# Fourteen turns per step of a gated-delta-rule kernel: from TensorE and ScalarE to DMA from buffer to buffer

## What is computed

```python
x = layernorm(x + attention(x))          # 16 key heads, 32 value heads, head size 128
x = layernorm(x + ffn(x))                # 12 experts of 256 x 640 x 256, all computed, weighed per token
# attention, per head pair: projection, causal convolution of 4 taps, silu, rms norm of q and k, then
def step(S, (q, k, v, g, beta)):         # over 512 tokens
    S = S * exp(g);  delta = (v - k @ S) * beta
    S = S + outer(k, delta);  return S, q @ S
# rms norm of the outputs, gate silu(z), projection W_out
```

## Time and profile before

| | us |
|---|---|
| median of 3 runs | 1567.07 (1566.12 to 1569.17) |
| the profiled execution's own time | 1565.32 |
| its span | 1563.5 |
| TensorE busy in the span | 1456.9 |
| VectorE busy | 1132.9 |
| ScalarE busy | 1064.0 |
| GpSimd busy | 701.1 |
| a walk of ORDER in the middle of the run | 67.6 |
| VectorE's copy of su 0 to St (line 895), first and last of 16 | 135.9 and 1135.8 |

### The profile page before, as it was taken

One profiled execution on the slowest core, in us unless ns is written; L12 is line 12 of the kernel. 1 busy time (PEld: TensorE's weight loads), 2 busy tenths in 40 slices (PEclk: granted clock), 3 DMA queues, 4 the chain that ended last, 5 costly groups with the idle time before them and its releaser, 6 DMA issues. The chain is left out here.

```text
span 1563.5 us, 38623 instructions
## 1 busy us (share of the span) xinstructions
PE 1456.9 (93%) x14982; PEld 1174.2 (75%) x14982; DVE 1132.9 (72%) x1970; ACT 1064.0 (68%) x2130; POOL 701.1 (45%) x613
## 2 busy tenths in 40 slices
PE   3589999999999999999999999999977899999994
PEld 2368898888988889888888989888864556656574
DVE  2588999999999999989999998999745332313214
ACT  2467878778787878778778887877635455464640
POOL 1243555454455544545454545545324344353530
PEclk9799999999999999999999999999998899999997
DMA  3000102021110202111020110202213111111100
GB/s 110 1 1 22 35 22 56 2 56 22 35 36 23 55 9 49 30 29 38 20 56 16 43 35 22 56 2 42 35 21 98 51 35 67 34 34 67 34 0 27
DMA packets 100713, 55.70 MB, mean 36 GB/s; under 512 B 74556, under 2 KB 93000, under 8 KB 100552
## 3 DMA queue, kind: packets, MB, share of 16 engines
q1 hardware_dynamic: 100552, 53.47, 13.9%
HBM read 35.62 MB, written 1.05 MB: 23 GB/s over the span
## 5 line engine op out<-in xcount | busy, mean ns | idle before, releaser
L819 DVE SCALAR_TENSOR_TENSOR con<-bank,taps,con 128x1022 f32<-128x1022 f32 (+2 forms) x192 | 245.2, 1277 | 24.0 <-ACT con L612 19.4
L1459 POOL TENSOR_TENSOR h<-h 128x512 f16<-128x512 f32 x120 | 146.2, 1226 | 177.8 <-ACT h L1278 171.5
L968 POOL TENSOR_TENSOR gl<-const_sb,gc 128x512 f16<-128x512 f32 x128 | 129.8, 1041 | 184.5 <-DVE gc L826 98.7
L1400 DVE SCALAR_TENSOR_TENSOR facc<-bank,gcol,facc 128x256 f32<-128x256 f32 x96 | 42.0, 479 | 224.4 <-PE bank L1193 224.4
L351 PE MATMUL bank<-x,qkv 128*128 128x512 f16 x768 | 184.6, 392 | 17.5 <-DVE con L819 13.6
L1179 PE MATMUL bank<-y,w 128*128 128x512 f16 x720 | 168.2, 384 | 6.4 <-ACT h L1278 3.3
L1277 ACT ACTIVATE h<-bank,b 128x512 f32<-128x512 f32 x120 | 82.5, 688 | 127.1 <-PE bank L1179 124.3
L1193 PE MATMUL bank<-w,h 128*128 128x256 f16 x1440 | 161.8, 275 | 2.4 <-DVE w L1323 2.4
L1193 PEld LDWEIGHTS bank<-w,h 128*128 128x128 f16 x1440 | 142.0, 99 | 23.1 <-DVE w L1323 2.6
L874 DVE TENSOR_TENSOR X<-X,bank 128x512 f16<-128x512 f16 x192 | 130.0, 683 | 32.4 <-PE bank L441 30.9
L351 PEld LDWEIGHTS bank<-x,qkv 128*128 128x128 f16 x768 | 75.0, 102 | 101.2 <-DVE con L819 14.9
(11 more groups left out here) (209 smaller groups left out, 3889.6 us busy)
## 6 DMA issues: line engine op xcount, KB each, us to landing
w<-in_w SPq DMA_DIRECT2D x24, 640.0 KB, 4.5
w_qkv<-in_W_qkvz SPq DMA_DIRECT2D x16, 512.0 KB, 3.9
w_z<-in_W_qkvz SPq DMA_DIRECT2D x16, 256.0 KB, 2.8
w_out<-in_W_out SPq DMA_DIRECT2D x16, 256.0 KB, 3.0
Z<-in_xT SPq DMA_DIRECT2D x1, 1024.0 KB, 5.3
y<-in_x SPq DMA_DIRECT2D x1, 1024.0 KB, 10.0
sqo<-oo SPq DMA_TRANSPOSE x64, 3.1
out_dram<-y SPq DMA_DIRECT2D x8, 128.0 KB, 1.8
```

The lines of the kernel that those rows point to most:

```text
L819: stt(out=out, in0=bank[:, 0:B, 0:S - k], scalar=taps[:, par, t, TAPS - 1 - k:TAPS - k], in1=out, op0=ALU.mult, op1=ALU.add).then_inc(tap_ ...
L968: last = tt(gl[:, g % 2, k].rearrange("p (m r) d -> p m r d", m=2), upper.unsqueeze(1).unsqueeze(1).broadcast_to([P, 2, R, P]), gc[:, par, ...
L1459: tt(h16[:, par, 1, t, at], h32[:, k % H32], h16[:, par, 0, t, at], ALU.subtract)\
```

## The change

1. Each x0 and turn becomes one DMA on SP's queue, from X0 to Z0 for eight matrices, with a semaphore `turned[h]` for each half. TensorE's transposes and ScalarE's copies of them go, and the PSUM banks that they took. All of Z0 is now written at each level. `p_level` and `apply_once` on TensorE wait for `turned`, and `start` on VectorE waits for it before X0 is written again.
2. The masks of levels 4 and 5 ("y") go from VectorE to ScalarE: with b = 32 the mask is constant along each run of 32 columns, with b = 64 along all 64, so a Copy with a scale from one mask column does it: two instructions of 8 x 32 columns at level 4 and one of 8 x 64 at level 5, for each half.
3. The copy of su's bank to St for chunk 0 goes from VectorE to ScalarE.
4. ORDER and BANK are new. Among other things "kk" 0 and 1, "aT" 0 and 1 and "decay" 1 end the walk (a = 2) where they were at its beginning or end with other a, "turn" (5, 1), "once" 2 and "split" z begin it, and the weights of head n are loaded up to three walks ahead (DEEP is 3, it was 2).

```diff
+TURNS = 16 * (LEVELS + 1)
+        turned = [sem(f"turned{h}") for h in range(2)]
@@ sync
+                def turn(h):
+                    sp.dma_start_transpose(out=Z0[:, 8 * h:8 * h + 8], in_=X0[:, 8 * h:8 * h + 8].rearrange("p u t -> p (u t)"))\
+                        .then_inc(turned[h], 16)
+
+                def turn_start(n, par, h):
+                    is_free(sp, n, ("st", 2 * h), ("st", 2 * h + 1))
+                    is_full(sp, n, ("Z", 2 * h, 1), ("Z", 2 * h + 1, 1))
+                    turn(h)
+
+                def turn_level(n, par, lh):
+                    l, h = lh
+                    is_free(sp, n, ("p", lh))
+                    turn(h)
+
+                run(sp, {"load": load, "oT": tail, "x0": turn_start, "turn": turn_level})
@@ tensor
-                def turn_start(n, par, h):
...
-                    is_free(pe, n, ("y", lh), ("turn", (l - 1, h)) if l else ("x0", h), taking=("p", lh))
+                    is_free(pe, n, ("y", lh), taking=("p", lh))
+                    pe.wait_ge(turned[h], TURNS * n + 16 * l + 16)
-                def turn_level(n, par, lh):
...
-                    is_free(pe, n, ("turn", (LEVELS - 1, g // 2)), taking=("once", g))
+                    pe.wait_ge(turned[g // 2], TURNS * n + TURNS)
@@ scalar
-                def turn_start(n, par, h):
...
-                def turn_level(n, par, lh):
+                def y_level(n, par, lh):
                     l, h = lh
...
+                    if l < LEVELS - 2:
+                        return
+                    is_full(act, n, ("y", lh), ("p", (l - 1, h)))
+                    pairs_of = 2 ** (LEVELS - 1 - l)
+                    for q in range(pairs_of):
+                        cols = slice(q * P // 2 // pairs_of, (q + 1) * P // 2 // pairs_of)
+                        last = do(Y[:, h, :, cols], at_bank("y", lh).rearrange("p (u k) -> p u k", u=8)[:, :, cols], ACT.Copy,
+                                  scale=ymask[:, l, cols.start:cols.start + 1])
+                    freed(last, "y", lh)
+                def su(n, par, c):
+                    if c == 0:
+                        is_full(act, n, ("su", c), ("ks", CH - 1, 1), ("qs", CH - 1, 1))
+                        freed(do(St[:].rearrange("p b r d -> p (b r d)"), at_bank("su", c), ACT.Copy), "su", c)
@@ vector
-                    is_full(dve, n, ("st", g), ("res", g, 1), ("turn", (LEVELS - 1, g // 2), 1))
+                    is_full(dve, n, ("st", g), ("res", g, 1))
+                    if after(n, 1):
+                        dve.wait_ge(turned[g // 2], TURNS * n)
+                    if l >= LEVELS - 2:
+                        return
-                    if c == 0:
-                        is_full(dve, n, ("su", c), ("ks", CH - 1, 1), ("qs", CH - 1, 1))
-                        freed(nc.vector.tensor_copy(St[:].rearrange("p b r d -> p (b r d)"), at_bank("su", c)), "su", c)
-                    else:
+                    if c:
                         is_full(dve, n, ("su", c), ("qs", c))
+                        if c == 1:
+                            is_free(dve, n, ("su", 0))
```

The new ORDER (BANK, which is new throughout, is left out):

```diff
+    (1, "aH", 0), (0, "turn", (5, 1)), (0, "split", "z"), (0, "once", 2),
+    (2, "split", "qkv"), (0, "res", 3), (0, "Z", 2), (1, "st", 0),
+    (1, "aH", 1), (1, "gl", 2), (1, "unit", 0), (1, "kk", 2),
+    (0, "once", 1), (0, "solve", 0), (1, "decay", 2), (1, "pT", 0),
+    (1, "st", 1), (1, "x0", 0), (1, "aT", 2), (0, "Z", 1),
+    (0, "su", 0), (0, "pdl", 0), (1, "aL", 0), (1, "unit", 1),
+    (1, "y", (0, 0)), (3, "load", "qkv"), (0, "sqo", 0), (1, "gl", 3),
+    (0, "ks", 1), (1, "aH", 2), (0, "kd", 1), (1, "decay", 3),
+    (0, "once", 3), (1, "turn", (0, 0)), (1, "p", (0, 0)), (1, "kk", 3),
+    (0, "solve", 1), (1, "aT", 3), (1, "sq", 0), (1, "st", 2),
+    (1, "pT", 1), (1, "aH", 3), (0, "qs", 1), (0, "sum", 0),
+    (0, "load", "out"), (0, "kd", 2), (0, "su", 1), (0, "Z", 3),
+    (1, "unit", 2), (1, "y", (1, 0)), (1, "st", 3), (0, "ks", 2),
+    (1, "x0", 1), (0, "sqo", 1), (1, "aL", 1), (0, "pdl", 1),
+    (1, "p", (1, 0)), (1, "y", (0, 1)), (0, "solve", 2), (0, "qs", 2),
+    (1, "turn", (1, 0)), (0, "sum", 1), (1, "y", (2, 0)), (1, "p", (0, 1)),
+    (1, "turn", (0, 1)), (0, "pdl", 2), (0, "su", 2), (1, "v", (1, 1)),
+    (0, "sqo", 2), (1, "p", (2, 0)), (1, "turn", (2, 0)), (1, "y", (1, 1)),
+    (0, "split", "out"), (0, "sum", 2), (2, "proj", 1), (1, "p", (1, 1)),
+    (0, "ks", 3), (1, "turn", (1, 1)), (1, "v", (1, 0)), (1, "y", (2, 1)),
+    (2, "tap", 1), (0, "qs", 3), (1, "turn", (2, 1)), (0, "solve", 3),
+    (1, "norm", 0), (2, "silu", 1), (0, "pdl", 3), (1, "p", (2, 1)),
+    (1, "pT", 2), (1, "y", (3, 0)), (0, "sum", 3), (1, "turn", (3, 0)),
+    (0, "sqo", 3), (1, "turn", (4, 0)), (2, "proj", 2), (2, "gc", 0),
+    (1, "y", (3, 1)), (1, "p", (3, 0)), (1, "unit", 3), (2, "tap", 2),
+    (1, "turn", (3, 1)), (0, "weigh", 0), (0, "weigh", 1), (2, "tok", 0),
+    (0, "power", 0), (2, "sq1", 1), (2, "tok", 1), (0, "oT", 0),
+    (0, "z", 0), (0, "z", 1), (1, "y", (4, 0)), (2, "silu", 2),
+    (0, "z", 2), (0, "high", 0), (1, "p", (3, 1)), (1, "p", (4, 0)),
+    (0, "oT", 1), (2, "proj", 3), (1, "turn", (5, 0)), (0, "high", 1),
+    (0, "z", 3), (2, "kT", 1), (1, "y", (5, 0)), (2, "tap", 3),
+    (2, "v", (0, 0)), (1, "y", (4, 1)), (2, "kT", 0), (0, "low", 0),
+    (2, "v", (0, 1)), (0, "weigh", 2), (1, "pT", 3), (2, "silu", 3),
+    (0, "low", 1), (1, "p", (5, 0)), (0, "weigh", 3), (2, "proj", 0),
+    (1, "kd", 0), (1, "p", (4, 1)), (1, "turn", (4, 1)), (2, "tap", 0),
+    (1, "aL", 2), (0, "oT", 2), (2, "gl", 0), (0, "high", 2),
+    (1, "res", 0), (0, "op", 0), (0, "high", 3), (1, "load", "z"),
+    (1, "once", 0), (1, "y", (5, 1)), (1, "res", 1), (0, "op", 1),
+    (2, "gl", 1), (2, "silu", 0), (2, "decay", 0), (1, "p", (5, 1)),
+    (1, "Z", 0), (2, "decay", 1), (2, "kk", 0), (2, "aT", 0),
+    (1, "aL", 3), (0, "low", 2), (0, "oT", 3), (2, "kk", 1),
+    (0, "low", 3), (2, "aT", 1), (1, "res", 2), (0, "op", 2),
     (0, "op", 3),
```

More of the change, by code:

```diff
@@ L37 @@
 ORDER = [
[11 rows of a table removed]
-    (1, "aH", 3), (2, "load", "qkv"), (1, "turn", (0, 0)), (1, "unit", 3),
[10 rows of a table removed]
[L60 to L65, removed]
@@ L66 @@
-    (1, "y", (5, 0)), (1, "p", (3, 1)), (2, "tap", 2), (2, "sq1", 1),
-    (0, "weigh", 0), (2, "tok", 0), (2, "tok", 1), (1, "turn", (4, 0)),
[5 rows of a table removed]
[L73 to L77, removed]
@@ L78 @@
-    (1, "res", 2), (1, "Z", 0), (1, "once", 2), (1, "kd", 1),
-    (2, "silu", 0), (1, "aL", 3), (0, "op", 2), (2, "decay", 1),
+    (1, "aH", 0), (0, "turn", (5, 1)), (0, "split", "z"), (0, "once", 2),
[4 more added lines that the diff above has]
+    (0, "su", 0), (0, "pdl", 0), (1, "aL", 0), (1, "unit", 1),
@@ L83 @@
 BANK = {
[11 rows of a table removed]
-    ("solve", 3): 7, ("turn", (3, 0)): 3, ("decay", 0): 4, ("y", (3, 1)): 2, ("pdl", 3): 7,
-    ("p", (4, 0)): 6, ("turn", (2, 1)): 5, ("norm", 0): 3, ("y", (5, 0)): 4, ("p", (3, 1)): 7,
-    ("tok", 0): 6, ("tok", 1): 5, ("turn", (4, 0)): 2, ("z", 0): 3, ("z", 1): 4,
[3 rows of a table removed]
-    ("once", 0): 2, ("p", (5, 1)): 5, ("res", 1): 7, ("op", 1): 6, ("turn", (5, 1)): 5,
-    ("res", 2): 4, ("Z", 0): 3, ("once", 2): 5, ("op", 2): 2, ("decay", 1): 5,
-    ("op", 3): 7,
+    ("once", 2): 7, ("res", 3): 5, ("Z", 2): 3, ("st", 0): 7, ("kk", 2): 2,
+    ("once", 1): 6, ("solve", 0): 4, ("decay", 2): 3, ("st", 1): 6, ("Z", 1): 5,
[15 rows of a table added]
 }
+TURNS = 16 * (LEVELS + 1)
 DEEP = max(a for a, *_ in ORDER)
@@ L311, in tail @@
                                            in_=oo16[:, g].rearrange("p k u d -> p (k u d)")).then_inc(oT_in[g], 16)
-                run(sp, {"load": load, "oT": tail})
+                def turn(h):
[10 more added lines that the diff above has]
+                run(sp, {"load": load, "oT": tail, "x0": turn_start, "turn": turn_level})
             @block.tensor
@@ L442, in p_level @@
                     filled(last, "p", lh)
-                def turn_level(n, par, lh):
-                    l, h = lh
-                    is_free(pe, n, ("p", lh), taking=("turn", lh))
-                    out = half16(take(n, "turn", lh))
-                    for j in range(8):
-                        last = turn(out[:, j], X0[:, 8 * h + j], ident16[:])
-                    filled(last, "turn", lh)
                 def residual(n, par, g):
@@ L556, in _ @@
                 run(pe, {"proj": proj, "norm": norm, "tok": tok, "v": turn_v, "kT": turn_k, "decay": decay_sum,
-                         "kk": products, "st": start, "x0": turn_start, "y": y_level, "p": p_level, "turn": turn_level,
+                         "kk": products, "st": start, "y": y_level, "p": p_level,
                          "res": residual, "once": apply_once, "Z": finish_z, "z": z, "ks": ks, "qs": qs,
@@ L668, in high_part @@
                     do(aH[:, 4 * g:4 * g + 4], aT[:, g % 2], ACT.Copy).then_inc(aH_ready, 1)
-                def turn_start(n, par, h):
```

(16 more changed lines are left out.)

## The result

The changed kernel takes 1598.01 us (1596.52 to 1599.04, 4 runs) against 1568.12 us (1566.12 to 1569.88) before: a ratio of 1.019, interval 1.0174 to 1.0206. It is 30 us slower, where 71 us less were forecast. The profiled execution has a span of 1595.9 us, 32.4 more than before.

A forecast was written before the change was run, and what follows sets the result against it. TensorE was taken as the bound: 61.3 + 1.4 (tap 3) + 0.2 (hops) + 0.1 = 63.0 us a walk, 64 us over 14 walks, plus 4 and 3 at the ends: 71 less, 1496 us. Range 1468 to 1548.

The forecast's parts named there:

- TensorE's list: Walks 0 to 13: TensorE sets the end; without 14 turn blocks its work falls from 67.5 to 61.3 us.
- ScalarE and the masks: Each walk: VectorE falls from 62.45 to 59.4 us; ScalarE gains 3.0, stands at 49 of 61 and hides it.
- Worth by themselves: nothing: Masks and su's copy moved to ScalarE gain no time alone, since TensorE is the bound.
- The order: New ORDER per walk: VectorE is late next, between y (3, 1) and proj 0, 13.6 us against TensorE's 12.2.
- The wait for tap 3: At proj 0, once a walk, TensorE waits 1.4 us for VectorE.
- The hops: From p by VectorE through DMA to the next p: tight ones cost 0.2 us a walk, bounds 0 to 5.4.
- The fit that the prediction quotes: DMA landing: about 2.0 us plus bytes at 436 GB/s, 2.6 us for 256 KB; the trace's 3.1 was used.
- The ends: Outside walks 0 to 13: walk 14 gains 4 us, walk -1 with the first inverse 3, walk 15 nothing.
- The clock, slower: Rival, chance 0.09: waits for landings drop TensorE's mean clock to 0.90, a walk of 69.7 us, time 1596.
- TensorE alone: Rival, chance 0.15: the new order leaves no wait, a walk of 61.4 us, time 1470.
- VectorE bound: Rival, chance 0.18: VectorE's 5.1 us a walk of waits for banks remain, a walk of 64.5, time 1519.
- Late landings: Rival, chance 0.13: landings typically 4.5 us cost about 3 us more, a walk of 66, time 1542.

The follow-up runs named there:

- masks_only: The kernel before with only the masks of levels 4 and 5 and su's first copy moved to ScalarE, old order and TensorE turns: 1567.73 us, 1.0008.
- masks_on_vector: gl_early with the masks of levels 4 and 5 back on VectorE: 1684.33 us, 1.0756 of the kernel before.
- gl_early: The changed kernel with GpSimd's gl 0, gl 1 and VectorE's gc 0 moved forward into GpSimd's idle time: 1553.21 us, 0.9917 of the kernel before.
- no_level_turns: The changed kernel without the twelve level turns, x0's DMAs kept, inverse not the reference's: 1578.87 us, 1.0083 of the kernel before.
- no_turns_gl_early: gl_early with no DMA from X0 to Z0 at all, Z0 filled once with a constant: 1525.35 us, 0.9734 of the kernel before.
- old_order_dma: The changed kernel with ORDER and BANK of before, oT entries moved behind their low: 1752.15 us, 1.119 of the kernel before.

## Why the prediction was wrong

**TensorE's list (change 1).** Right. 67.5 was to fall to 61.3; in the last window above, 63.57 less gaps of 2.5 us, read off block by block from start to start, is 61.1.

**ScalarE and the masks (changes 2 and 3).** The size was right: 49.15 us against 49 (rows below). "Worth by themselves: nothing" is right in the old order (masks_only) and right for the reason given. In the new order ScalarE doesn't hide the masks quite: kT 0 stands 0.47 us a walk for one, 0.6 from start to start, for which the sum had nothing. I did write that they count because VectorE would stand at 62.4; that measured VectorE by its sum. masks_on_vector says that position, not sum, was the point: 6 us a walk of waits, 8 with the clock.

```profile
L677 ACT ACTIVATE Y<-bank,ymask 128x256 f16<-128x256 f32 x64 | 27.1, 487 | 0.0
L677 ACT ACTIVATE Y<-bank,ymask 128x512 f16<-128x512 f32 x32 | 21.9, 685 | 0.0
```

**The order (change 4): the step that failed.** The prediction priced weigh at 1.05 us and VectorE at 59.4 a walk, durations read in the old order, and carried them into a new one without asking what GpSimd does at that moment. I followed TensorE, VectorE, ScalarE and SP through the new ORDER, but not GpSimd, which at 34 of 67 us looked like no bound. It needn't be one to hold up another engine. Weigh 2 and 3 stand on VectorE's path for TensorE: tap 3, weigh 2, the read of p (5, 0), on which res 0 and turn (5, 0) wait, weigh 3, the read of p (4, 1), on which turn (4, 1) waits. Their spans are 3.89 + 2.33 = 6.2 us in place of 2.3. gl_early takes 3.5 of these 4.0 us away, and 3.0 reach the end of the walk: 68.3 to 65.3 (45 us of the time).

The 5.3 us a walk that the forecast was short by are then these 3.0, 1.5 of hops beyond the 0.2 that it took (below), and 0.8 that stay without any turn, ScalarE's mask ahead of kT 0 among them.

The wait for tap 3, forecast at 1.4 us from start to start, was 0.79 idle and 0.95 from start to start in the walk without turns, and 0.15 idle after the change, where TensorE comes late itself.

**The hops.** "I take 0.2 us a walk", with bounds of 0 to 5.4. Measured 1.3 (after against no_level_turns) to 1.7 (gl_early against no_turns_gl_early), within the bounds, but the value taken was too near the lower end. The median landing was 3.1 as taken. (The fit that the prediction quotes beside it from the Trainium skill, "DMA: Bandwidth & Descriptors", Anatomy of one DMA, was measured on GpSimd's DMA queue. These transfers are SP's, none of them landed in under 3.0 us, and the sum rightly went by the trace.) What was missed is that a hop begins with VectorE's read, and that once 0, which I gave no price, waits for turn (5, 0). The walks in gl_early lie between 63.6 and 66.7 us, while those without turns are all alike: it is the turns' landings that spread them.

**The ends.** The head's first inverse was to gain 3 us and walk 14 was to gain 4. The start lost 11.6. There p stood 2.0 and 2.8 us for x0's DMA, and the granted clock was 0.66 between 80 and 100 us (before: 1.00), which is 1.2 GHz for much of it:

```profile
80.00:100.00 20.00, 10.41 (x103) 7.72 (x104) 10.99 (x17) 5.49 (x13) 7.64 (x8) 0.66 0.51 93
```

But taking the x0 DMAs away brought only 3.7 us from the first write of X0 on, so this is not the main part, as said above. Walk 14 is 58.5, without level turns 55.6, before 53.5: 3 of the 5 us lost are hops. Moving gl lengthens it again, to 60.7 (57.7 without level turns, 55.6 without any). The 6.1 us behind the last St copy are there without any turn as well (1522.9 - 1088.6 = 434.3). 1.2 of them lie ahead of the layer norm that ends the attention part (its first rstd) and 4.9 from there to the end, where the code is the same: this stretch took 382.1 us before and in masks_only, 384.7 in gl_early and old_order_dma, 387.0 after. Neither the turns nor the new order alone goes with that, and the cause is open.

**The rivals.** *The clock, slower* gave 1596, within 2 us of the measured time, and fell all the same: the clock was 1.00 in the walks. That it came so near is luck. Its mechanism is real, but in other kernels of this case: masks_on_vector and old_order_dma. *TensorE alone* fell with the 0.79. *VectorE bound* named the right engine, by its total and not by a stretched instruction, and *Late landings* a part of 1.3 to 1.7 us a walk where 3 was said. No rival held two engines contending. The range ended at 1548 since I took every bound from durations in the old order.

## What to carry to other kernels

A duration is valid beside the neighbours that it was measured with: when steps are reordered, follow also the engine that is half idle, and mark each VectorE instruction with two SBUF inputs that comes to stand beside a GpSimd instruction. Look for an engine's idle stretch (here 22.5 us of GpSimd) and put its work there before anything else is tuned. A short instruction that others wait for is priced by what stands ahead of it in its queue, not by its length.

## What the runs showed of the hardware

- Four VectorE instructions of 128 elements with two SBUF tensors: 1.13 us alone, 1.63 to 2.33 beside aL or low, 3.89 beside gl. Taps and masks, with a PSUM operand, weren't slowed. The splits of the weights, with two SBUF inputs too, moved both ways: z's mean went from 1090 ns to 763 (681 at the least), qkv's from 1218 to 1393, with 2172 at the most.
- SP's transposes of 256 KB landed in 3.1 us in the median with four and a half times as many of them (224 + 64 in place of 64), and the turns in 5.0 at worst (before, oT: 4.9); oT's own median went from 3.1 to 3.4. The DMA queue's share rose from 13.9% to 36.3%.
- TensorE kept 2.4 GHz in walks with three waits of 1.0 to 1.5 us (1.00 at 62.4 of 67.9 us busy), and was granted a mean of 0.93 in walks with waits of up to 7.7 us (67.5 of 78.7 us busy). In masks_on_vector each walk has waits of 3.65 and 2.4 us and some of 1.0 to 1.6, and the clock was 1.00 in four walks, 0.98 in two and 0.93 to 0.96 in eight: with nearly the same waits it falls in one walk and not in the next, and the walks in which it falls are 3.3 to 3.9 us longer. The Trainium skill ("TensorE: Matmul & The Clock Gate", HAM oscillation) tells of a matmul kernel that is throttled again at each of its waits for DMA, all longer than 1.5 us; the walks after the change show that waits of about 1 us for DMA don't bring it about.
